# Attention: the values of two groups of heads at a time, and a stationary operand of 128 rows for the spreading of the sums

## What is computed

```python
NUM_HEADS = 16; WINDOW = 128; PERSIST = 16
q = (x @ Wq).reshape(B, S, H, hd)          # hd = 32
kv_latent = x @ Wkv
k = (kv_latent @ Wk).reshape(B, S, H, hd)
v = (kv_latent @ Wv).reshape(B, S, H, hd)
mask = (ki <= qi) & ((qi - ki < WINDOW) | (ki < PERSIST))
scores = jnp.einsum('bqhd,bkhd->bhqk', q, k) * scale
scores = jnp.where(mask[None, None], scores, jnp.finfo(scores.dtype).min)
attn = jax.nn.softmax(scores, axis=-1)
out = jnp.einsum('bhqk,bkhd->bqhd', attn, v).reshape(B, S, D)
return out @ Wo
```

## Time and profile before

| | |
|---|---|
| median of 3 runs | 4574.59 us (4567.81 to 4588.4) |
| the profiled execution, its own time | 4576.1 us |
| its span, first to last instruction | 4574.2 us |
| mean granted clock of TensorE | 0.958 |
| PE busy over the span | 4213.9 us (92%) |
| DVE, ACT, POOL busy | 2097.7, 1663.7, 1220.5 us |

### The profile page before, as it was taken

The page is one execution under the profiler, slowest core; times in us unless marked ns, Lnnn a source line. Parts: engine busy times, 40 slices in busy tenths (PEclk is TensorE's granted clock), DMA queues, the critical chain, the costliest instruction groups (busy, mean ns, idle before and its releaser), DMA issues. The chain is left out here.

```text
span 4574.2 us, 68643 instructions
## 1 busy us (share of the span) xinstructions
PE 4213.9 (92%) x23045; PEld 3557.8 (78%) x23046; DVE 2097.7 (46%) x4006; ACT 1663.7 (36%) x3234; POOL 1220.5 (27%) x1809
## 2 busy tenths in 40 slices
PE   6966888879999999999997999998799999999998
PEld 5854667668989888888886777776578888788887
DVE  4457666644444444444444554453333333333333
ACT  2214766643343434343332333332222222222222
POOL 0012444434444444444442233333100000000000
PEclk8877999989999999999998999998899999999999
DMA  5776666635555556565554443342423222221221
GB/s 199 284 231 162 128 136 128 114 96 118 113 126 120 130 112 130 114 131 118 124 116 130 168 150 121 133 134 71 143 76 104 97 87 75 97 99 63 97 81 48
DMA packets 351750, 560.87 MB, mean 123 GB/s; under 512 B 33057, under 2 KB 198593, under 8 KB 347330
## 3 DMA queue, kind: packets, MB, share of 16 engines
q1 hardware_dynamic: 282770, 394.19, 29.3%
q0 software_dynamic: 68784, 164.10, 16.9%
HBM read 383.84 MB, written 174.34 MB: 122 GB/s over the span
## 5 line engine op out<-in xcount | busy, mean ns | idle before, releaser
L1206 POOL DMA_INDIRECT acc_d<-e_yw,e_to x208 | 336.1, 1616 | 342.4 <-ACT e_yw L1339 330.6
L2244 POOL DMA_DIRECT2D out<-d_res x32 | 17.3, 542 | 1305.3 <-DVE d_res L2476 1305.3
L2423 DVE TENSOR_TENSOR d_h<-d_sg,d_psU 128x512 f32<-128x512 f32 x144 | 99.1, 688 | 520.1 <-PE d_psU L107 461.7
L972 ACT ACTIVATE a_pr<-a_sm,a_nmax 128x272 f32<-128x272 f32 x512 | 264.0, 516 | 164.3 <-DVE a_nmax L1027 122.5
L105 PE MATMUL e_psG<-e_gu,e_xT 128*128 128x352 f32 x832 | 286.3, 344 | 8.5 <-DVE e_xT L1393 8.5
L1401 DVE TENSOR_TENSOR e_h<-e_sg,e_psU 128x352 f32<-128x352 f32 x208 | 108.4, 521 | 387.3 <-ACT e_sg L1352 383.9
L1027 DVE CUSTOM_DVE_ANT_0 a_sm<-a_psS,a_mask 128x272 f32<-128x272 f32 x512 | 213.1, 432 | 156.7 <-PE a_psS L867 134.8
L107 PE MATMUL e_psU<-e_gu,e_xT 128*128 128x352 f32 x832 | 268.8, 323 | 0.0
L105 PE MATMUL e_psU<-e_gu,e_xT 128*128 128x352 f32 x832 | 268.5, 323 | 0.0
L106 PE MATMUL e_psU<-e_gu,e_xT 128*128 128x352 f32 x832 | 268.3, 323 | 0.0
L106 PE MATMUL e_psG<-e_gu,e_xT 128*128 128x352 f32 x832 | 267.8, 322 | 0.0
(11 more groups left out here) (423 smaller groups left out, 11901.8 us busy)
## 6 DMA issues: line engine op xcount, KB each, us to landing
d_gu_raw<-in_wgu SPq DMA_DIRECT2D x144, 512.0 KB, 3.2
qk_d<-f_qk SPq DMA_DIRECT2D x32, 1024.0 KB
a_q<-qk_d SPq DMA_DIRECT2D x96, 256.0 KB
a_k<-qk_d SPq DMA_DIRECT2D x96, 256.0 KB
e_rawgu<-in_w_gate SPq DMA_DIRECT2D x32, 704.0 KB
e_rawgu<-in_w_up SPq DMA_DIRECT2D x32, 704.0 KB
b_gu_raw<-in_wgu SPq DMA_DIRECT2D x40, 512.0 KB, 3.9
xT_d<-f_xT SPq DMA_DIRECT2D x16, 1024.0 KB
```

Of the source, the lines that this page charges most:

```text
L972: act.activation(pr[half][:, h % HH, :], sm[s % SR][:, :], ACT.Exp, bias=nmax[s % SR][:, :], scale=-1.0, accum_out=rs[u % 2][:, h:h + 1]). ...
L1206: pool.indirect_dma_start(env.acc_d, bass.IndirectOffsetOnAxis(ap=to[:, :].bitcast(U32), axis=0), yw[:, :], None, compute_op=ALU.add).then ...
L2423: ins = dve.tensor_tensor(hv[q % 2][:, :], sg[q % 2][:, :], psU[:, :], ALU.mult)
```

## The change

The values of groups 0 and 1 are made together in step 12, those of 2 and 3 together in step 20, where each group had a step of its own before (8, 12, 16, 20). The spreading moves from step 19 to 20, behind the values; all that hangs on it moves one step back: `pers_values` to 21, `inverse_out` to 21, `divide` to 22, `out_hi` and `out_lo` to 23, `project` to 26 to 29, `finish` to 30. The table `sel` gets 128 rows in place of 16; the added rows are zero, and the matmuls of the spreading take all 128 rows of `a_xT`, of which rows 16 and up are zero too.

```diff
-        sel = sb("a_sel", [NH, NGR, GH, HD])
+        sel = sb("a_sel", [P, NGR, GH, HD])
...
                     ins = pe.matmul(psR[:, g, :], sel[:, g, :, :].rearrange("p j d -> p (j d)"),
-                                    xT[u % 2][0:NH, 2 * P:3 * P], start=True, stop=True)
+                                    xT[u % 2][:, 2 * P:3 * P], start=True, stop=True)
...
-                for g in range(NGR):
+
+                for g in range(1, NGR, 2):
                     if (u := tile_of(s, GH * g + GH - 1 + LAG)) is not None:
+                        values(u, g - 1)
                         values(u, g)
                 if (u := tile_of(s, X_AT)) is not None:
                     turn_sums(u)
-                if (u := tile_of(s, X_AT + 2)) is not None:
+                if (u := tile_of(s, X_AT + 3)) is not None:
                     spread(u)
-                if (u := tile_of(s, X_AT + 3)) is not None:
+                if (u := tile_of(s, X_AT + 4)) is not None:
                     pers_values(u)
                 for c in range(KC):
-                    if (u := tile_of(s, X_AT + 8 + c)) is not None:
+                    if (u := tile_of(s, X_AT + 9 + c)) is not None:
                         project(u, c)
...
-                if (u := tile_of(s, X_AT + 3)) is not None:
+                if (u := tile_of(s, X_AT + 4)) is not None:
                     inverse_out(u)
-                if (u := tile_of(s, X_AT + 5)) is not None:
+                if (u := tile_of(s, X_AT + 6)) is not None:
                     out_hi(u)
...
-                if (u := tile_of(s, X_AT + 4)) is not None:
+                if (u := tile_of(s, X_AT + 5)) is not None:
                     divide(u)
-                if (u := tile_of(s, X_AT + 5)) is not None:
+                if (u := tile_of(s, X_AT + 6)) is not None:
                     out_lo(u)
-                if (u := tile_of(s, X_AT + 12)) is not None:
+                if (u := tile_of(s, X_AT + 13)) is not None:
                     finish(u)
```

## The result

The changed kernel takes 4558.07 us (median of 6 runs, 4553.71 to 4562.09), the kernel before 4579.26 in the same session (6 runs, 4567.81 to 4588.4). The ratio is 0.9956, interval 0.9941 to 0.9971. So the forecast's direction holds and its size doesn't: 4 us less was predicted, 21 were found.

A forecast was written before the change was run, and what follows sets the result against it. The prediction took a ring of PE, DVE and ACT as the bound, not PE alone. Its walk of four pieces summed to 17.18 us a tile against 17.31, 4 us less over 31 tiles: 4571 us, range 4540 to 4602.

The forecast's parts named there:

- a ring of PE, DVE and ACT: First layer's attention: PE scores, DVE masks, ACT exponentiates, PE turns; with three steps of lookahead, the layout of heavy steps counts.
- Rival A: PE is the bound in the attention; all 2.3 us a tile come off, 71 us: 4504 us; chance 0.10.
- The delayed signals: Values inside POOL's DMA-issue runs were read as making DVE and ACT take PE's results late, idle 0.95 and 0.98 us.
- Rival B: Delayed signals were the bound and bunching costs nothing; 0.84 us a tile comes off, 26 us: 4549 us; chance 0.13.
- (a): First values of step 20 to the score behind the persistent values, PE-bound: 3.37 us.
- (b): From the score behind the persistent values to the projection, a chain over all three engines: 3.56 us, before 3.85.
- (c): Projection to the score behind it, PE-bound: 5.44 us, before 4.50.
- The two stalls: PE's waits for ACT's copy of the sums (0.84 us) and DVE's division (0.70 us), 1.54 us, predicted to go.
- (d): From the score behind the projection to the values of step 20, DVE-bound: 4.81 us, bounds 4.3 to 5.3.
- The padding's price: The spreading's eight matmuls fall from 1.08 to 0.92 us with 128 rows: 0.16 us less a tile, bounds nothing or 0.30.
- C: The pair of step 12 falls into POOL's run, margin about 0.6 us: 40 to 108 us slower, 4611 to 4680; chance 0.10.
- D: Bunching costs 0.5 us a tile or over more than the walk shows, DVE starved: 4590 us and above; chance 0.07.

The follow-up runs named there:

- e5: Kernel before, with only POOL's scatter runs made to wait until the values of group 0 and of group 2 are done: 4547.86 us, ratio 0.9942.
- e6: Changed kernel, with POOL's second run held until the turned sums are copied, so that it lies over the pair of step 20: 4659.72 us, ratio 1.0195.
- e8: Kernel before, with POOL's runs behind the values and the padded operand, without pairs and moves: 4534.25 us, ratio 0.9909.
- e9: Kernel before, with the groups paired at steps 12 and 20 and the padded operand, the spreading and all behind it unmoved: 4558.36 us, ratio 0.9951.
- e2: Changed kernel without the padding, the spreading's operand back at 16 rows: 4563.47 us, ratio to the kernel before 0.9950.
- e1: Kernel before, with the padded operand of the spreading alone, everything at its old step: 4573.44 us, ratio 0.9973.
- c0: Kernel before, unchanged, run once more: 4579.36 us, period 17.75 us a tile.
- e7: Changed kernel, with groups 0 and 1 at step 9 instead of 12 and POOL's first run behind them: 4624.45 us, ratio to the kernel before 1.0102.
- e4: Kernel before, with the pairs of groups alone (steps 12 and 20), 16 rows, the spreading and all behind it unmoved: 4646.49 us, ratio 1.0157.

## Why the prediction was right or wrong

- **The reading of the profile** (a ring of PE, DVE and ACT, in which the place of heavy steps counts) held. Rival A fell: PE is busy 350.59 of the 400 us from 500 to 900, 88%, as before, and of the 2.3 us of stalls and switches the period gave back 0.44.
- **The delayed signals** were a reading then and are shown now by e5 and e6: taking the values of groups 0 and 2 out of POOL's runs removes the three idle pieces with PE's work unchanged, and laying a run over a pair brings one of 1.96 us. Rival B had this mechanism right, and its time, 4549, lies 9 us from the measured 4558.07 where the forecast's 4571 lies 13 us from it; the time alone doesn't choose between them. What fails is its second half, that bunching costs nothing: e8, with the padding in and the groups apart, has a period of 16.05 us; e9, which differs from it by the pairs and by POOL's waits alone, 16.94; the change 16.87. So the bunching takes at least 0.8 us a tile, 25 us: e8 still has one delay, which the other two haven't, and they have the division's wait (0.70 us) off their path and two of four changes of shape less.
- **Pieces (a), (b), (c)** measured 3.39, 3.49 and 5.43 against 3.37, 3.56 and 5.44. The two stalls went, as said, and most of their time came back, as said.
- **Piece (d)** is the term of the sum that was mis-sized: 4.81 predicted, 4.49 measured. The five operations of DVE take 2.03 us, as taken; the handovers from one engine to the next are 0.03 to 0.12 us shorter than the rows from which I took them: score to maximum 0.44 (0.53), maximum to exponential 0.47 (0.56), exponential to values 0.14 (0.26; perhaps a waiting PE pays no change of shape on top, which no run isolates), and the exponential behind the sums' copy starts after 0.37 (0.40). Over 31 tiles that is 10 us, and 0.32 of the 0.38 us by which the tile shown is shorter than the walk.
- **The padding's price**, 0.16 us a tile, was right for step 20 (0.17); from e2 to the change the period falls by 0.10 us on average, in most tiles by 0.2 (three tiles of the change ran partly at a lower clock). In the old place, among full-row matmuls, it is 0.38 us (e5 to e8). Against the kernel before e1 gives 12 us, of which a part can be the clock's: from 500 to 900 us it is 1.00 with the padding and 0.95 in c0.
- **The base** is a step that I didn't see as one: the sum was made against the mean of one execution. That mean holds the short last period of 15.04 us; the 30 whole tiles average 17.38, and it is beside these that the walk of a tile in the stream belongs. And the delays hit that kernel unevenly: at full clock its tiles took 16.89 to 17.46 us, c0's 17.31 to 17.91, and e5's, without the three idle pieces, 16.44 to 16.77. Against c0's 17.75 the same walk (17.18) would have been 0.57 us a tile, 18 us.
- **The sum of it.** 4 us were predicted and 21 found. Of the 17 between them (d) explains 10; 5 are the kernel before, whose median was 4574.59 when I made the forecast and 4579.26 in the comparison; the rest is within the scatter of its runs. The mechanism was right, and the sizes that were off are (d) and the base. The stated range, 4540 to 4602, took in the walk and rival B alike, so that the measured time lies in it speaks for neither; the pieces do.
- **Rivals C and D.** C did not happen: its margin was 0.84 us (702.28 to 703.12), where I had put 0.6, and e6 puts its price, at full clock, at the lower bound (1.3 us a tile). D did not happen either; DVE starves in two pieces, of which the forecast had named the one under the values of step 20 (1.94 us).

Left open: why a result of PE is handed on late when values run inside POOL's DMA issues, and why in some tiles of e7 also without them (whether the 32-column shape, the number of matmuls or the run's length matters wasn't tried), and what in e4, e6 and e7 makes the clock fall. e9 says that the spreading's shape is enough to tip it in e4; no run here isolates more. Nor was a kernel tried whose POOL run clears the values of group 3 as well, which e8's doesn't.

## What to carry to other kernels

Where a matmul's result is taken late although its engine is recorded as done, look for what else was being issued at the time, and move that first: here two waits on POOL gave 0.58%, as much as the whole reordering of PE (0.50% without the padding), and with the padding a shorter period than the change (16.05 against 16.87 us). Work that is bunched to save changes of shape starves the engines that live on a short lookahead behind it, and that can take back what it saves. And a forecast of half a per cent needs more than one execution of the kernel before: if the tiles of one trace vary by 1 us, as here (16.9 to 18.4), their mean is no base. Compare tiles at the same granted clock, or two effects are read as one.

## What the runs showed of the hardware that was not expected

- When values run inside POOL's indirect-DMA issues, the maximum behind them starts late, about when an issue or the run ends: 0.52 us behind the score's recorded end (median of 27, kernel before), 1.18 (31, e1) and 1.96 in e6's tile, where 0.15 is usual outside; parted, the kernel gains 0.58% (e5).
- Four matmuls with 16 rows cost 0.37 us more than with 128 zero-padded rows, when they stand among full-row matmuls (0.58 + 1.09 against 0.49 + 0.81), and 0.17 behind 32-column ones.
- The granted clock fell to 0.50 for some 7 us in most tiles of a kernel (e4), and stayed at 1.00 in nearly all tiles of one that differs only by the padding (e9). The difference is 2% of the kernel.
